# Softplus on one activation table with its last sum on TensorE; in the entry, the last rounding of the weights on ScalarE and the first two table steps

## Time and profile before

| | us |
|---|---|
| median of 3 runs | 3593.43 |
| lowest and highest | 3587.59, 3596.02 |
| the profiled execution | 3589.46 |
| its span | 3587.7 |
| busy TensorE, VectorE, ScalarE, GpSimd | 3152.9, 2548.6, 1766.2, 1209.0 |

### The profile page before, as it was taken

How to read it: one execution, slowest core, us unless ns; L and a number is a source line. 1 busy time by engine, 2 the same in 40 slices (tenths; PEclk the granted TensorE clock), 3 DMA queues, 4 the chain that set the end, 5 groups by cost and what they waited for, 6 DMA issues and landing times. The chain is left out here.

```text
span 3587.7 us, 34351 instructions
## 1 busy us (share of the span) xinstructions
PE 3152.9 (88%) x10665; PEld 1524.1 (42%) x10677; DVE 2548.6 (71%) x4823; ACT 1766.2 (49%) x3354; POOL 1209.0 (34%) x962
## 2 busy tenths in 40 slices
PE   3750599999999799999999999899899988999963
PEld 3330244444444344444444444344444444444442
DVE  8768899999999756666666666643421156899954
ACT  4748476666666434343443434344310115888821
POOL 0433699999999101101000000021378020000014
PEclk9975799999999999999999999999999998999987
DMA  7115435253342222222211111243632012000047
GB/s 263 48 58 161 154 97 145 96 138 106 113 131 82 71 92 83 68 71 82 69 58 56 59 59 53 97 138 122 217 122 101 10 53 71 1 1 1 25 137 238
DMA packets 201398, 336.22 MB, mean 94 GB/s; under 512 B 25664, under 2 KB 76224, under 8 KB 198080
## 3 DMA queue, kind: packets, MB, share of 16 engines
q1 hardware_dynamic: 187984, 300.27, 25.6%
q0 software_dynamic: 12208, 33.57, 3.3%
q10 hardware_dynamic: 1024, 0.20, 0.0%
HBM read 219.26 MB, written 114.69 MB: 93 GB/s over the span
## 5 line engine op out<-in xcount | busy, mean ns | idle before, releaser
L1282 POOL TENSOR_TENSOR sc_dBu<-sc_dtu,xa 128x1024 f32<-128x1024 f32 x256 | 540.6, 2136 | 41.6 <-DMA sc_dtu<-scan_dtu 32.6
L1192 PE MATMUL y_ps<-sc_g,ident 128*128 128x512 f32 x1024 | 475.9, 600 | 18.1 <-POOL sc_g L1270 11.7
L1565 ACT ACTIVATE c_p<-c_ps,c_sm 128x512 f32<-128x512 f32 x256 | 195.8, 774 | 367.7 <-DVE c_sm L1618 367.7
L1306 DVE TENSOR_TENSOR_SCAN sc_dA<-sc_dA,sc_dBu 128x1024 f32<-128x1024 f32 x160 | 365.1, 2282 | 6.7 <-POOL sc_dBu L1282 6.7
L1246 ACT ACTIVATE sc_dA<-sc_dt,a_neg 128x511 f32<-128x511 f32 x512 | 329.6, 676 | 11.0 <-DVE sc_g L1306 9.8
L1192 PEld LDWEIGHTS y_ps<-sc_g,ident 128*128 128x128 f32 x1024 | 190.0, 190 | 255.7 <-issue 169.4
L1606 DVE SCALAR_TENSOR_TENSOR xa<-c_ps,c_sm,xa 128x512 f32<-128x512 f32 x256 | 192.1, 751 | 148.6 <-PE c_ps L1518 129.1
L1518 PE MATMUL c_ps<-c_wo,c_oT 128*128 128x512 f32 x512 | 246.5, 605 | 2.3 <-DVE xa L1606 1.6
L1500 PE MATMUL c_ps<-u,c_wq 128*128 128x512 f32 x512 | 233.3, 599 | 4.5 <-DMA c_wq<-in_c_wq_dram 4.5
L1528 PE MATMUL c_ps<-c_kT,c_qT 128*128 128x512 f32 x512 | 237.0, 606 | 0.0
L1545 PE MATMUL c_ps<-c_pT,c_v 128*128 128x512 f32 x512 | 231.7, 595 | 0.0
(11 more groups left out here) (545 smaller groups left out, 6063.0 us busy)
## 6 DMA issues: line engine op xcount, KB each, us to landing
kv_w<-in_c_wkv_dram SPq DMA_DIRECT2D x32, 512.0 KB, 4.0
cross_keys<-kv_out SPq DMA_DIRECT2D x64, 256.0 KB, 2.0
cross_values<-kv_out SPq DMA_DIRECT2D x128, 128.0 KB, 2.0
c_kT<-cross_keys SPq DMA_DIRECT2D x64, 256.0 KB
c_rk<-cross_rk SPq DMA_DIRECT2D x64, 256.0 KB
c_v<-cross_values SPq DMA_DIRECT2D x64, 256.0 KB, 2.6
expert_rows<-e_yt SPq DMA_DIRECT2D x63, 256.0 KB, 2.0
xa<-scan_bc SPq DMA_DIRECT2D x48, 256.0 KB, 7.7
```

Of the source, the lines that this page charges most:

```text
L1192: ins = pe.matmul(yps[:, k % 2, :], ident[:], g[:, c % GS, n, :], start=False, stop=(m == NCH - 1 and n == NG - 1))
L1282: pool.tensor_tensor(dBu[:, c % 3], spread(dtu[:, k % DT, :], NG), bc[:, m * NG:(m + 1) * NG, :], ALU.mult).then_inc(s_dBu, 1)
L1306: dve.tensor_tensor_scan(to.rearrange("p n s -> p (n s)"), dA[:, c % 2].rearrange("p n s -> p (n s)"), dBu[:, c % 3].rearrange("p n s -> p ...
L1565: ins = act.activation(pr[:, j, :], ps[:, SB + j, :], ACT.Exp, scale=rq[:, j:j + 1], bias=bias[:, j:j + 1], accum_out=l[:, j:j + 1])
```

## The change

In `entry`:
- The last pass of `quantized` (line 506) leaves VectorE for the four chunks; ScalarE does it in two passes (`rounded`: add the rounding constant, subtract it again into `wq`). ScalarE's next chunk waits for that.
- GpSimd's marking of earlier occurrences no longer waits for the first chunk, and ScalarE's 32 counting passes are spread between the chunks (6, 10, 16).
- `locu` and `tot` are made before the loop over tiles instead of behind it. GpSimd makes the first two table steps as soon as they and the zeroed table are there, and takes its second maximum over partitions behind these.
- In the loop ScalarE copies 12 of the 16 tiles and VectorE 4.

The other sections make 13, 6 and 11 table steps instead of 14, 6 and 12.

In `softplus`:
- ScalarE loads one activation table at the start, a set that holds both exponential and logarithm.
- The clamp goes from `v` into a new bf16 tile `r` (subtract and max, then min), and the scale moves into ScalarE's bias pass.
- The sum with `w` (line 1002) leaves VectorE: TensorE adds `w` and the logarithm by two float32 products with the identity for each 512 columns, four a pair, in two new PSUM buffers; the products of the projection keep two of their four buffers.
- VectorE's order puts the last pair's step of a batch behind the first lost part of the next. ScalarE's rounding of the fourth pair moves behind the third logarithm, and it waits for the stores of its own pair of batch b-2 only.

The core of the diff:

```diff
+CELL_STEPS = (2, 15, 21, ST)
...
 def entry(...)
-    copied_by_act = [t for t in range(NT) if t % 3]
+    copied_by_act = [t for t in range(NT) if t % 4]
...
             @block.gpsimd
...
                 pool.wait_ge(s_eq, 1)
-                pool.wait_ge(s_done, 1)
-
                 pool.affine_select(out=low, in_=eq[:], compare_op=ALU.is_gt, fill=0.0, base=0,
                                    pattern=[[0, ST], [-1, P]], channel_multiplier=1).then_inc(s_low, 1)
+                pool.wait_ge(s_fill, 80)
+                pool.wait_ge(s_locu, 2)
+                add_cells(pool, rmw, s_sum, 0, CELL_STEPS[0])
                 pool.wait_ge(s_mx2, 1)
                 pool.partition_all_reduce(mxa[:], mx[:], P, ABSMAX)
...
             @block.scalar
...
+                def rounded(i, n, out):
+                    act.wait_ge(s_done, i + 1)
+                    act.activation(n, n, ACT.Copy, bias=MAGIC).then_inc(s_up, 1)
+                    act.wait_ge(s_up, i + 1)
+                    act.activation(out, n, ACT.Copy, bias=-MAGIC).then_inc(s_q, 1)
+
+                def counted(lo, hi):
+                    for i in range(lo, hi):
+                        ins = act.activation(low[:, i, :], low[:, i, :], ACT.Square, accum_out=cnt[:, i:i + 1])
+                    return ins
+
+                def chunk(i):
                     if i >= 2:
-                        act.wait_ge(s_done, i - 1)
+                        act.wait_ge(s_q, i - 1)
                     integer(i, near[:, i % 2, :], raw[:, i * WC:(i + 1) * WC], W_IN)
...
+                chunk(0)
+                chunk(1)
...
+                act.wait_ge(s_low, 1)
+                counted(0, 6)
+                rounded(0, near[:, 0, :], wq[:, 0, :])
+                chunk(2)
+                counted(6, 16)
+                rounded(1, near[:, 1, :], wq[:, 1, :])
+                chunk(3)
+                rounded(2, near[:, 0, :], wq[:, 2, :])
+                counted(16, ST).then_inc(s_cnt, 1)
+                rounded(3, near[:, 1, :], wq[:, 3, :])
+                act.wait_ge(s_q, HC)
                 integer(HC, near[:, 0, 0:CT * KW], cw[:].rearrange("p a n -> p (a n)"), W_CONV)
...
             @block.vector
...
-                    own.after(dve.scalar_tensor_tensor(out=n, in0=r, scalar=winv[:, w:w + 1], in1=n, op0=ALU.mult,
-                                                       op1=ALU.add))
-                    dve.tensor_scalar(out, n, MAGIC, MAGIC, ALU.add, ALU.subtract).then_inc(s_done, 1)
+                    dve.scalar_tensor_tensor(out=n, in0=r, scalar=winv[:, w:w + 1], in1=n, op0=ALU.mult,
+                                             op1=ALU.add).then_inc(s_done, 1)
...
+                dve.wait_ge(s_cnt, 1)
+                own.after(dve.tensor_scalar(cnt[:], cnt[:], 0.0, None, ALU.is_gt))
...
+                dve.tensor_copy(locu[:], locf[:]).then_inc(s_locu, 1)
+                dve.wait_ge(s_tot, 1)
+                dve.tensor_copy(tot[:].rearrange("p i e -> p (i e)"), ip[:, 2, 0:ST * NE0]).then_inc(s_locu, 1)
...
+                quantized(HC, small, flat_cw, W_CONV)
+                dve.wait_ge(s_done, HC + 1)
+                dve.tensor_scalar(flat_cw, small, MAGIC, MAGIC, ALU.add, ALU.subtract)
...
 def in_proj_conv(...)
-                add_cells(pool, rmw, s_sum, 0, CELL_STEPS[0])
+                add_cells(pool, rmw, s_sum, CELL_STEPS[0], CELL_STEPS[1])
 def x_proj(...)
-                add_cells(pool, rmw, s_sum, CELL_STEPS[0], CELL_STEPS[1])
+                add_cells(pool, rmw, s_sum, CELL_STEPS[1], CELL_STEPS[2])
 def softplus(...)
+        r = sb("sf_r", [P, CT, S], BF16)
-        dps = ctx.enter_context(nc.psum_tensor("sf_ps", [P, 4, 2, S], F32))
+        dps = ctx.enter_context(nc.psum_tensor("sf_ps", [P, 2, 2, S], F32))
+        lps = ctx.enter_context(nc.psum_tensor("sf_lps", [P, 2, 2, S], F32))
...
-                add_cells(pool, rmw, s_sum, CELL_STEPS[1], CELL_STEPS[2])
+                add_cells(pool, rmw, s_sum, CELL_STEPS[2], CELL_STEPS[3])
...
             @block.tensor
...
+                def logs(b):
+                    for i in range(PAIRS):
+                        n = b * PAIRS + i
+                        if n >= 2:
+                            pe.wait_ge(s_dt, n - 1)
+                        pe.wait_ge(s_c, n + 1)
+                        pe.wait_ge(s_ln, n + 1)
+                        for h in range(2):
+                            j = 2 * i + h
+                            pe.matmul(lps[:, n % 2, h, :], ident[:], w[:, j, :], start=True, stop=False)
+                            ins = pe.matmul(lps[:, n % 2, h, :], ident[:], e[:, b % 2, j, :], start=False, stop=True)
+                        ins.then_inc(s_add, 1)
+
+                products(0)
+                for b in range(NB):
+                    if b + 1 < NB:
+                        products(b + 1)
+                    logs(b)
...
             @block.scalar
...
+                def rounded(b, i):
+                    n = b * PAIRS + i
+                    act.wait_ge(s_mm, n + 1)
+                    if b >= 2:
+                        act.wait_ge(s_st[b % 2 * PAIRS + i], 32 * (b // 2))
...
+                act.preload_act_table_set("natural_log_exp_and_others")
...
-                            ins = act.activation(v[:, b % 2, j, :], v[:, b % 2, j, :], ACT.Identity, bias=dtb[:, j:j + 1])
+                            ins = act.activation(v[:, b % 2, j, :], r[:, j, :], ACT.Identity, scale=S_DT, bias=dtb[:, j:j + 1])
...
                     if b + 1 < NB:
-                        rounded(b + 1)
+                        for i in range(PAIRS - 1):
+                            rounded(b + 1, i)
                     for i in range(PAIRS):
+                        if b + 1 < NB and i == PAIRS - 1:
+                            rounded(b + 1, i)
                         act.wait_ge(s_c, b * PAIRS + i + 1)
                         act.activation(two(e, b, i), two(e, b, i), ACT.Ln, bias=1.0).then_inc(s_ln, 1)
...
             @block.vector
...
-                        own.after(dve.tensor_scalar(x, x, MAGIC - 128.0, MAGIC + 127.0, ALU.max, ALU.min))
-                        dve.tensor_scalar(x, x, MAGIC, S_DT, ALU.subtract, ALU.mult).then_inc(s_t, 1)
+                        n, x = b * PAIRS + i, r[:, 2 * i:2 * i + 2, :]
...
+                        own.after(dve.tensor_scalar(x, two(v, b, i), MAGIC, -128.0, ALU.subtract, ALU.max))
+                        dve.tensor_scalar(x, x, 127.0, None, ALU.min).then_inc(s_t, 1)
...
+                def stepped(b, i):
+                    n = b * PAIRS + i
+                    dve.wait_ge(s_add, n + 1)
+                    dve.scalar_tensor_tensor(out=two(v, b, i), in0=two(v, b, i), scalar=0.0, in1=lps[:, n % 2], op0=ALU.max,
+                                             op1=ALU.add).then_inc(s_dt, 1)
...
                 clamped(0)
                 for b in range(NB):
                     for i in range(PAIRS):
...
+                        if b and i == 1:
+                            stepped(b - 1, PAIRS - 1)
+                        lost(b, i)
                     if b + 1 < NB:
                         clamped(b + 1)
-                    for i in range(PAIRS):
...
-                        own.after(dve.tensor_tensor(c, two(e, b, i), c, ALU.add))
...
+                    for i in range(PAIRS - 1):
+                        stepped(b, i)
+                stepped(NB - 1, PAIRS - 1)
```

More of the change, by code:

```diff
@@ L593, in _ @@
                         dve.tensor_tensor(mx[:, W_OUT:W_OUT + 1], mx[:, 4:5], mx[:, 5:6], ALU.max).then_inc(s_mx2, 1)
-                dve.wait_ge(s_cnt, 1)
-                own.after(dve.tensor_scalar(cnt[:], cnt[:], 0.0, None, ALU.is_gt))
-                dve.wait_ge(s_sp, 1)
-                own.after(dve.tensor_scalar(tmp[:], locf[:], spare[:], -1.0, ALU.subtract, ALU.mult))
-                own.after(dve.tensor_tensor(tmp[:], tmp[:], cnt[:], ALU.mult))
-                own.after(dve.tensor_tensor(locf[:], locf[:], tmp[:], ALU.add))
-                dve.tensor_copy(locu[:], locf[:])
-                dve.wait_ge(s_tot, 1)
-                dve.tensor_copy(tot[:].rearrange("p i e -> p (i e)"), ip[:, 2, 0:ST * NE0])
                 dve.tensor_scalar(dsk[:], dsk[:], S_U, None, ALU.mult)
@@ L894, with softplus @@
 PAIRS = CT // 2
-def softplus(nc, xa, u, dtq, dwq, dtb, kk, soft, bcd, rmw):
+def softplus(nc, xa, u, dtq, dwq, dtb, kk, soft, bcd, rmw, ident):
     with ExitStack() as ctx:
@@ L959, in _ @@
+                for i in range(PAIRS):
+                    rounded(0, i)
                 for b in range(NB):
```

96 lines of the change are left out of this document (43 added, 53 removed).

## The result

The changed kernel takes 3573.82 us (median of 6 runs, 3558.49 to 3576.35), the kernel before beside it 3594.72 (6 runs, 3587.59 to 3601.88): ratio 0.9942, 95% interval 0.9922 to 0.9962. That is 20.9 us less, between 14 and 28; the forecast was 21.1 less. The profiled execution took 3576.35 us, its span is 3574.5.

What follows compares the result with a forecast made beforehand. VectorE was taken to bound softplus and nearly fill the entry's loop; 17.3 us off softplus and 3.8 off the entry sum to 21.1, so the median goes from 3593.43 to 3572 us, range 3562 to 3582.

Steps and rivals of the forecast that it cites:

- VectorE sets softplus, and its period is 21.6: Softplus: VectorE's work alone sets the length of a batch, which falls from 27.43 to 21.6 us.
- First period 23.0, last batch 21.2: Softplus: first batch 23.0 us with waits for TensorE's first pairs at half clock; last batch, without a clamp, 21.2.
- Head 16.2: Softplus, ahead of the first lost part: 16.2 us for 16.4, the one table load running beside the first products.
- TensorE at full clock fits, 18 us of 21.6: Softplus: sixteen sum products plus 3.4 us of projection take 18 us a batch at full clock, within VectorE's 21.6.
- Rival (a): Softplus: TensorE stays at half clock, 32 us a batch, and bounds the stage at 145 us; 3613 us, chance 0.03.
- Rival (b): Softplus: TensorE's clock falls in every batch, slowing each first pair, three times 2 us more; 3578 us, chance 0.14.
- (c): Softplus: tables still switched before each exponential and logarithm, eight loads, ScalarE the bound at 23.3 us a batch; 3579, chance 0.05.
- (e): Softplus: GpSimd's table steps end the stage, at 10.0 us a step for 8.0, 112 us; 3581 us, chance 0.05.
- Entry, 3.8 us less: Entry: VectorE and ScalarE end near 95.5, level with GpSimd's all-reduce at 95.4, so 3.8 us shorter.
- the loop starts 3.1 us earlier: Entry: VectorE's loop over tiles starts at 73.2 for 76.30, four passes leaving and the locu and tot block coming ahead.
- the second change of code: Entry, GpSimd: going from add to all-reduce costs 7.0 us again, as before the first add; bounds 0 and 7.
- Rival (d): Entry: GpSimd ends it late, through slowed transfers or a longer code change; at 4 us more, 3576 us, chance 0.08.

Runs made afterwards that it cites:

- e11: e3 plus ten products nobody reads, on TensorE while it rests ahead of softplus's first pair; 3560.73 us, ratio to the kernel before 0.9906.
- e6: The changed kernel without the one instruction that loads a common table for exponential and logarithm; 3566.23 us (1 run), 3580.99 for the kernel before.
- e9: The changed kernel with w added to the sum once more, six TensorE products a pair for four; 3602.72 us (1 run), 3594.43 for the kernel before.
- e3: The changed kernel with GpSimd's marking again waiting for VectorE's first chunk and ScalarE's counting later; 3556.81 us, timed again 3552.72, ratio then 0.992.
- e2: The kernel before with only the changed softplus, and twelve GpSimd steps in it; 3560.53 us, ratio to the kernel before 0.9941.
- e7: The changed kernel with the sum of logarithm and lost part back on VectorE; 3572.82 us (1 run), 3594.43 for the kernel before.

## Why the prediction was right, and where it wasn't

**VectorE sets softplus, and its period is 21.6.** Right: 21.60 and 21.58. The parts: line 1002 gone, the second clamp 0.43, and the PSUM operand +0.00 for the 0.03 taken.

**First period 23.0, last batch 21.2.** 23.13 and 20.83. The waits of the first batch are 2.05 + 2 x 0.95 = 3.95 for 1.8 + 2 x 1.1 = 4.0; e11, at full clock, shows that about 3 us of it is the low clock. One term of it doesn't follow as written: four products at half clock from 7.1 on end at 14.2 and not at 13.7. Measured is 13.67, as the clock rose within the fourth.

**Head 16.2.** This term was mis-sized: "the one load at the start runs beside the first products" was right, but I took 0.2 off for it. Before, the exponentials' own load of 1.28 us stood ahead of the first exponential and thus of the first lost part; the head lost 1.16 (14.04 to 12.88), and has it back in e6 (14.29). That is 1.0 of the 1.1 us by which softplus gained more than forecast.

**TensorE at full clock fits, 18 us of 21.6.** Right for four products; but comparing TensorE's busy time with the period was too simple. The 18 also holds 3.4 us of projection as read at a clock of 0.53, which takes 2.2 in the changed kernel (from 301.06 on), and even so e9 shows less room than I counted, since the projection and the roundings stand in series with the sums: an estimated 1.3 to 3 us instead of 3.6. Rival (a), the 16 products and the 3.4 over 27 us, would have decided sooner than I put it: 20.6 us of sums already give back the whole gain (stage 124.41 for 122.45).

**Rival (b), the clock falls in every batch.** It had 0.14 and came in part: behind the first batch the clock is low again in batch three alone in the changed kernel, in two of the three later batches in e3, and in all three in e2 and e11. The Trainium skill's rule of bursts that start at half clock after a gap ("TensorE: Matmul & The Clock Gate", "HAM oscillation — how this bites in real kernels") agrees with most bursts of e2 and e11, and not with batch two of the changed kernel, which came behind a pause as long and ran at full clock; in e2's second batch the clock fell only in the second product (a row of 1.29 us for the 2.04 of half clock). The price is not the 2 us a batch that I gave it: with the deferred step as cover it is nothing for 3.4 us at half clock (21.58), and 0.5 to 0.8 for 6.5 (e2 22.11, e11 22.39).

**Rivals (c) and (e).** One load, so (c) fell; its price by e6 is 8.3 us, forecast 6.4. The eleven steps' last one ends at 353.0, 11 us ahead of the last product's end (364.23), so (e) fell.

**Entry, 3.8 us less.** Wrong: 0.7, or 0.1 to 0.9 by all traces of this entry. The step that failed is "the loop starts 3.1 us earlier". The change takes the wait ahead of the marking away, and of that the prediction says nothing: it is a move, of a 3.84 us pass beside VectorE, and I counted it at nothing without a word. It took back 3.46 us on VectorE; the rest of the sum held (e3: 72.59 for the loop's start, 4.4 us less by section for 4.1 worked out). GpSimd's terms held too: two steps 15.9 us (75.53 to 91.44) for 15.8, the second change of code 6.10 for 7.0, which the Trainium skill's 6 in "GPSIMD Engine Reference", "Instruction dispatch", meets better. They began 3.4 us late (75.53 for 72.1), as `tot` was late, and the all-reduce ended 2.5 late (97.93 for 95.4). Rival (d) is there in little: in_proj waits for GpSimd, by some 0.3 us over ScalarE's copy at 98.02 with its 0.94.

**Sum.** The difference of the medians (20.9) came out 0.2 us from the forecast one, and that is luck: by sections 0.7 and 18.4 make 19.1, two errors of +1.1 and -3.1, and a measurement that can tell some 7 us. In the profiled execution the gain was 21.9 us at mid-span (SyncE's same load of `c_wo`, 1765.59 for 1787.44) and 13.2 at the end, through sections that nobody changed.

## What to carry to other kernels

Before moving an operation, look for what runs beside it at its new place, and if it is GpSimd reading SBUF beside VectorE with two SBUF inputs, count the two in series. When an engine takes over work in a ring of engines that wait for one another, compare the period with the chain around the ring and not only with each engine's busy time; one run with half as much work again shows how much room is left. A stage can be measured to tenths, or to half a microsecond, by its own rows where the whole time can't tell several microseconds.

## What I had not expected of the hardware

- VectorE's pass of 128x2048 with two SBUF inputs took 5.81 us for 2.35 beside GpSimd's `affine_select`, which took 5.96 for 3.84. Beside VectorE's `BATCH_NORM_STATS2`, where it ran before, neither was longer (3.84, and 2.46 for four of these as without it).
- GpSimd paid at each change between all-reduce and add, not once: 5.9 to 6.7 us towards the all-reduce, 6.8 to 7.6 towards the add.
- The clock rose 3.2 us into the sums' first products in e3 and 6.5 us into them in the changed kernel, and each kernel repeated its own value within 0.2 us in a second trace.
- Sections that nobody touched differ from trace to trace: in_proj with x_proj from 162.5 to 167.0 us, and the changed kernel's lead over before went from 21.9 to 13.2 us behind the middle of the span. Single whole times, such as e7's, can't be read to less than that.
